# Attention stage of a float32 decoder block: the output projection moved between the K and V projections, and GpSimd's low part of y moved ahead of its two sums

## The reference, cut to what matters

```python
R = (_time_interp(x, EPS_R) @ Wr.T + br)
K = (_time_interp(x, EPS_K) @ Wk.T + bk)
V = (_time_interp(x, EPS_V) @ Wv.T + bv)
e = jnp.exp(jnp.clip(W + K, -20.0, 10.0))           # W: decay by distance to the end
past_attention = jnp.cumsum(e * V, axis=1)
past_energy = jnp.cumsum(e, axis=1)
eu = jnp.exp(jnp.clip(U + K, -20.0, 10.0))
A = shift(past_attention) + eu * V
B = shift(past_energy) + eu
out = (jax.nn.sigmoid(R) * (A / B)) @ Wo.T + bo
```

## Time and profile before

| | |
|---|---|
| median of 3 runs | 1364.01 us (1363.24 to 1364.49) |
| the profiled execution | 1365.01 us, its span 1363.1 us |
| attention stage | from about 17 to about 765 us of the span |
| busy over the span | PE 97%, DVE 81%, ACT 60%, POOL 47% |
| busy in tile 4 (382.7 to 472.1 us) | PE 89.27, DVE 82.84, ACT 57.15, POOL 37.30 of 89.40 us |
| granted TensorE clock, mean | 0.996 |

### The profile page before, as it was taken

How to read it: one execution, slowest core, us unless ns; L and a number is a source line. 1 busy time by engine, 2 the same in 40 slices (tenths; PEclk the granted TensorE clock), 3 DMA queues, 4 the chain that set the end, 5 groups by cost and what they waited for, 6 DMA issues and landing times. The chain is left out here.

```text
span 1363.1 us, 19357 instructions
## 1 busy us (share of the span) xinstructions
PE 1323.4 (97%) x6330; PEld 1099.5 (81%) x6330; DVE 1097.3 (81%) x1782; ACT 819.0 (60%) x1555; POOL 635.5 (47%) x558
## 2 busy tenths in 40 slices
PE   6899999999999999999999989999999899999998
PEld 5677788887888878888887778888888778888886
DVE  6999999989999899999999766665555777777774
ACT  5866666666666666566566454444446366666664
POOL 4665344343443434434334553444445565555551
PEclk9999999999999999999999999999999999999999
DMA  9000101001001110010050464444443312222212
GB/s 340 21 12 21 62 32 40 24 31 62 11 20 62 31 62 0 31 62 0 26 200 1 160 237 145 150 141 142 167 152 118 126 37 93 92 92 92 93 62 93
DMA packets 54540, 113.92 MB, mean 84 GB/s; under 512 B 2769, under 2 KB 7121, under 8 KB 52561
## 3 DMA queue, kind: packets, MB, share of 16 engines
q1 hardware_dynamic: 54480, 113.22, 23.3%
HBM read 88.05 MB, written 25.17 MB: 83 GB/s over the span
## 5 line engine op out<-in xcount | busy, mean ns | idle before, releaser
L827 POOL TENSOR_TENSOR a_ss<-a_ss,a_eu 128x512 f32<-128x512 f32 x64 | 82.5, 1290 | 270.8 <-DVE a_ss L634 270.8
L494 ACT ACTIVATE k_or_row<-bank 128x512 f32<-128x512 f32 x192 | 115.1, 599 | 53.3 <-PE bank L82 49.3
L616 DVE SCALAR_TENSOR_TENSOR bank<-bank,k_or_row 128x510 f32<-128x510 f32 x192 | 132.5, 690 | 15.2 <-ACT k_or_row L494 10.0
L832 POOL TENSOR_TENSOR a_sv<-a_sv,a_euv 128x512 f32<-128x512 f32 x64 | 82.6, 1291 | 119.2 <-DVE a_sv L651 119.2
L514 ACT ACTIVATE bank<-bank,a_nbr 128x510 f32<-128x510 f32 x64 | 42.2, 660 | 119.2 <-DVE bank L616 119.2
L401 PE MATMUL bank<-a_wo_hi,a_y_hi 128*128 128x512 f32 x256 | 100.4, 392 | 0.0
L401 PE MATMUL bank<-a_wo_hi,a_y_lo 128*128 128x512 f32 x256 | 99.7, 389 | 0.0
L401 PE MATMUL bank<-a_wo_lo,a_y_hi 128*128 128x512 f32 x256 | 99.6, 389 | 0.0
L1543 POOL TENSOR_TENSOR b_cx_lo<-b_cx,b_cx_hi 128x512 fp32r<-128x512 f32 x32 | 40.6, 1297 | 114.0 <-ACT b_cx_hi L1220 114.0
L836 POOL TENSOR_TENSOR a_y_lo<-a_yy,a_y_hi 128x512 fp32r<-128x512 f32 x64 | 85.9, 1342 | 2.0 <-ACT a_y_hi L537 2.0
L634 DVE TENSOR_TENSOR_SCAN a_ss<-a_mask,a_ee 128x514 f32<-128x514 f32 x64 | 79.6, 1244 | 2.2
(11 more groups left out here) (246 smaller groups left out, 4723.5 us busy)
## 6 DMA issues: line engine op xcount, KB each, us to landing
xres<-in_x SPq DMA_DIRECT2D x8, 1024.0 KB, 5.3
x_after_attention<-xres SPq DMA_DIRECT2D x8, 1024.0 KB, 4.3
xin<-x_after_attention SPq DMA_DIRECT2D x8, 1024.0 KB, 5.6
b_ct<-in_ctx_t SPq DMA_DIRECT2D x8, 1024.0 KB, 6.1
b_cx<-in_ctx SPq DMA_DIRECT2D x8, 1024.0 KB, 7.9
xres<-x_after_attention SPq DMA_DIRECT2D x8, 1024.0 KB, 5.6
x_after_cross<-xres SPq DMA_DIRECT2D x8, 1024.0 KB, 4.4
xin<-x_after_cross SPq DMA_DIRECT2D x8, 1024.0 KB, 5.6
```

Of the source, the lines that this page charges most:

```text
L494: sc.activation(u3[:, :, 1:], ps[m][:, :, :], ACT.Copy, scale=MIX[m]).then_inc(left[m], 1)
L616: ve.scalar_tensor_tensor(out=ps[m][:, :, 0:T - 1], in0=ps[m][:, :, 1:T], scalar=1.0 - MIX[m], in1=u3[:, :, 0:T - 1], op0=ALU.mult, op1=AL ...
L827: gp.tensor_tensor(ss3[:, :, 0:T], ss3[:, :, 0:T], eu[:, :, :], ALU.add).then_inc(b_done, 1)
L832: gp.tensor_tensor(sv3[:, :, 0:T], sv3[:, :, 0:T], euv[:, :, :], ALU.add).then_inc(a_done, 1)
```

## The change

TensorE's order within a chunk goes from K, V, R, output to K, output, V, R. The exceptions are chunk 2 of each tile (whose output opens the accumulator banks that the residual of the tile before must have left) and the last chunk of all: they keep K, V, R, output. The turn stays at the end of the chunk. GpSimd makes the low part of y for chunk g-1 before the two sums of chunk g, and not after them.

```diff
+            def drain(i, c):
+
+                if c >= LAG:
+                    output(i, c - LAG)
+                elif not is_first(i):
+                    output(i - 1, HC + c - LAG)
+
...
                 for c in range(HC):
-                    for m in WM:
-                        project(m, i, par, c)
+                    late = c == 2 or is_last(i) and c == HC - 1
+                    project("k", i, par, c)
+                    if not late:
+                        drain(i, c)
+                    project("v", i, par, c)
+                    project("r", i, par, c)
                     if is_last(i) and c == HC - 1:
...
-                    if c >= LAG:
-                        output(i, c - LAG)
-                    elif not is_first(i):
-                        output(i - 1, HC + c - LAG)
+                    if late:
+                        drain(i, c)
...
                     if c == 1 and not is_last(i):
                         rstd_of(i + 1)
+                    if c > 0 or not is_first(i):
+                        y_rest(g - 1, (c - 1) % HC)
                     below(g)
                     above(g)
-                    if c > 0 or not is_first(i):
-                        y_rest(g - 1, (c - 1) % HC)
```

## The result

The changed kernel takes 1419.93 us (median of 4 runs, 1418.25 to 1420.87) against 1363.81 us for the one before: a ratio of 1.0405, 95% interval 1.0386 to 1.0425. It is slower by 56 us; 1419 was predicted. The span of its profiled execution is 1417.6 us, 54.5 us over the old one.

A forecast was written before the change was run, and what follows sets the result against it. TensorE and VectorE were both taken to bound attention, VectorE alone after the change. Clashes with GpSimd's low part summed to 55.2 us on the profiled 1365.0, giving 1420.2; less 1.0 for the median, 1419 us, range 1410 to 1432 (8 in 10: 1368 to 1432).

The forecast's parts named there:

- VectorE is nearly as late as TensorE: Attention: VectorE needs 88.25 us a tile, TensorE 88.97, so VectorE has under 0.1 us a chunk to spare.
- the price: VectorE time lost per chunk when GpSimd's low part meets a clip or scan: 1.09 us, bounds 0.97 and 1.29.
- The low part comes up between the clips, and costs 1.09 us a chunk.: GpSimd's low part starts between VectorE's clips L628 and L630; L630 loses 1.09 us, or else the scan 0.97.
- The sum, piece by piece.: Attention, between VectorE's quotients: tiles 1 to 6 +45.9 us, tile 7 +5.5, last chunk +1.1, tile 0 +2.7; total 55.2.
- the floor: VectorE's time for one attention tile when it never waits for TensorE, only for ScalarE's reciprocal: 88.25 us.
- The last chunk adds one meeting, +1.1 us.: End of tile 7: one more clash of the low part with VectorE's work lengthens the last chunk by 1.1 us.
- TensorE's order costs nothing beside the meeting.: Attention: if VectorE's own pace sets the end, the new order of TensorE's blocks costs and brings nothing.
- TensorE then idles for some 0.4 to 0.8 us in most chunks, at V.: Attention, with VectorE slowed to 12.1 us a chunk: TensorE waits 0.4 to 0.8 us before V in most chunks.
- A wait for the low part (L845): Sign that the forecast is wrong: TensorE waiting for GpSimd's low part of y before its output matmuls.
- The cheaper meeting: Rival: low part comes up once the first scan runs, costing 0.6 us a chunk; +27 us, 1391 us, chance 0.15.
- The waiting chunk 2: Rival: no costly meeting; TensorE waits 1.26 us at V of chunk 2; about +4.6 us, 1369 us, chance 0.10.
- The faster case: Rival: VectorE loses nothing to GpSimd, and 5 us of attention's waits of V go; 1359 us, chance 0.08.

The follow-up runs named there:

- pool_only: Kernel before with only GpSimd's half of the change: y's low part ahead of the two sums, TensorE's order old; 1417.36 us, ratio 1.0388.
- tiny_rest: Changed kernel, both new orders kept, with y's low part made for only 8 of 512 columns; 1367.99 us, ratio 1.0027.
- tiny_old: Kernel before, all orders old, with y's low part made for only 8 of 512 columns; 1358.51 us, ratio 0.9955.
- rest_after_scan: Changed kernel, but GpSimd waits for VectorE's first scan before making y's low part; 1381.03 us, ratio 1.0128.
- order_only: Changed kernel with y's low part put back behind the two sums, so only TensorE's order is new; 1644.52 us, ratio 1.206.

## Why the prediction was right

- *VectorE is nearly as late as TensorE* (88.25 against 88.97 us a tile). Shown by two sizes of the price: with 1.1 us more a chunk nearly all of it appears in the time, with 0.53 us a third of the full loss and not half.
- *The low part comes up between the clips, and costs 1.09 us a chunk.* Shown: 12.11 us with a turn, 11.28 without, that is 1.10 us over the old steps, or 0.98 where the scan pays. I had named both victims; that it would be the scan in 19 chunks, at the smaller price of the two, I had not.
- *The sum, piece by piece.* Tiles 1 to 6: 706.07 - 118.92 = 587.15 us, forecast 585.8. Tile 7: 789.21 - 706.07 = 83.14, forecast 83.8 (78.31 + 5.5). Up to the quotient of 1.0: +2.64 us, forecast +2.7, although this execution's first K began 0.6 us earlier, so that the piece is really 3.2. (Before, the splits met the clips in five chunks of tile 0, 0.2 to 0.6, and not in four.) Tile 4 alone: 96.92 us; the floor and eight prices make 88.25 + 8 x 1.09 = 96.97. That the whole sum, 55.2 us, lies within 1 us of what was measured is in part luck: the misses of +1.3 us in tiles 1 to 6, -0.7 in tile 7 and -1.1 in the last chunk cancel. The +1.3 are themselves a difference: VectorE waits 2.6 us for V in these tiles, a term that the sum had put at nothing, and 15 of the 47 meetings fall on the scan at 0.98 us, which makes them 1.3 us cheaper together.
- *"The last chunk adds one meeting, +1.1 us."* This step failed. From the quotient of 7.7 to the last one it was 12.59 us and is 12.57, though the clip took 1.50 us. Both traces show where it went: behind the chunk VectorE waits for TensorE's bias products, before for 1.98 us and now for 0.88 us, 1.10 us less. TensorE and not VectorE set that last step.
- *TensorE's order costs nothing beside the meeting.* Nearly so. The ratios 1.0388 and 1.0405 overlap, but the traces show VectorE waiting for V in chunk 3 of six tiles, 3.8 us that pool_only does not have. In the other chunks of tiles 1 to 6 VectorE alone sets the pace. Without a meeting the order costs 9.5 us, as tiny_rest against tiny_old shows.
- *"TensorE then idles for some 0.4 to 0.8 us in most chunks, at V."* Wrong. I applied the shorter distance from V of chunk 1 to V of chunk 2 only in the rival. With more room in the other chunks TensorE runs ahead through chunks 3 to 7, and pays most of what it owes at chunk 2 at once. The time is nearly the same, since VectorE sets it. A wait for the low part (L845), one of my signs of being wrong, did come once, for 0.8 us in tile 1.
- *Rivals.* The cheaper meeting needed the low part to come up after the scan had begun; it never did. Forced behind the first scan (rest_after_scan) it gave 1381 us, not the 1391 worked out. The waiting chunk 2 was real, 1.2 to 2.0 us a tile with next to no meeting (tiny_rest), and beside the meeting it is hidden but for the 3 us above. The faster case has nothing for it: with the meeting all but removed the order is still slower than the same kernel in the old one.

The Trainium skill's rule ("SBUF — State Buffer", section "SBUF: two separate sides") holds here in that a first comer keeps the other out. Its list of who competes fits the scan, which reads two SBUF tensors; the clip reads one, and whether it ran in a two-port mode no trace shows, but it was held up as the rule has it for that mode. The time kept out is shorter than by the rule: in chunk 4.5 1.24 us of GpSimd's instruction were left when the clip came up, and it lost 1.10 us; no clip of this kernel lost more than 1.12.

## What to carry to other kernels

Before moving a GpSimd instruction, write down which VectorE instructions will run in the 1.3 us after its new start; here two-source SBUF work and SBUF-to-SBUF `tensor_scalar` paid, and work with an operand in PSUM did not (all 192 mixes took 0.68 to 0.70 us, before and after). An engine at 81% over the span can be the bound of its stage: sum its steps where it waits for nobody, and compare them with the other engine's. Where TensorE waits need not be where the time is lost; undo one half of the change to see which half it is.

## What the runs showed of the hardware that was not expected

- TensorE's clock fell after waits that come in every chunk. In order_only, with waits of 3.3 us a chunk, the twelve matmuls behind a wait ran mostly at 1.2 GHz (granted clock 0.61 over 4.4 us), 1.7 us more a chunk, and the mean clock of the whole span is 0.944 instead of 0.996. Over the 53 waits of the stage it is 80 of the 85 us by which this kernel was slower than expected. In the changed kernel the mean is 0.989, and waits of 3 us at chunk 2 were followed by the lower clock in six tiles of eight.
- A GpSimd instruction that comes up 0.09 us ahead of the second of two back-to-back clips (477.11 and 477.20 us), while the first still runs (476.87 + 0.42 = 477.29), gets in between them. It did so in 43 of the 44 chunks in which it came up 0.08 to 0.10 us ahead (not in 0.1). Where it came up 0.02 us ahead of that clip (415.84 and 415.86 us), the clip went first and the scan waited, as in all 11 chunks with 0.02 or 0.03 us; but in pool_only GpSimd was first in three of 11 such chunks. So a tenth of a microsecond decides who pays, and near it the order is not certain. The loss is about the same either way, 1.10 or 0.98 us.
- 45 of 64 L639 were slow, and 54 of 64 with TensorE in the old order; who pays shifts with the moment at which ScalarE's high part is done, the total hardly. Where V was late (chunk 3 of six tiles) the low part came up 0.24 us behind the second clip, and the scan paid.
